# Four-layer gated cross-attention with expert feed-forwards: half-width value product and router bias on VectorE in layer 1, plain gathers with VectorE adds after layers 1 and 2, and three products of ones ahead of each head output of layer 1

## The reference

```python
x = x + tanh(g_xattn[l]) * xattn_l(layernorm(x), ctx_768)
x = x + tanh(g_ffn[l]) * ffn_l(layernorm(x))
```

## Time and profile before

| | us |
|---|---|
| median of 3 runs (lowest, highest) | 1220.69 (1220.15, 1220.71) |
| the profiled execution | 1213.56 |
| its span, first to last instruction | 1211.8 |
| TensorE busy (weight loads apart) | 1092.0 |
| VectorE, GpSimd, ScalarE busy | 876.1, 757.9, 577.1 |

### The profile page before, as it was taken

How to read it: one execution, slowest core, us unless ns; L and a number is a source line. 1 busy time by engine, 2 the same in 40 slices (tenths; PEclk the granted TensorE clock), 3 DMA queues, 4 the chain that set the end, 5 groups by cost and what they waited for, 6 DMA issues and landing times. The chain is left out here.

```text
span 1211.8 us, 23059 instructions
## 1 busy us (share of the span) xinstructions
PE 1092.0 (90%) x6989; PEld 772.5 (64%) x6990; DVE 876.1 (72%) x2216; ACT 577.1 (48%) x1248; POOL 757.9 (63%) x1010
## 2 busy tenths in 40 slices
PE   7999897889989999998899998999999999999553
PEld 5666563555556678956667766778976666666413
DVE  3899855888798668666678777666767777767496
ACT  2555432555455334444455544224435555554465
POOL 2455522764578864379998887853319988886213
PEclk7999996998898799999999999899999999999865
DMA  7996020000000015601111100023501111100002
GB/s 198 387 402 259 1 80 1 1 2 1 1 17 21 30 48 156 172 12 19 18 21 21 22 23 25 32 62 102 136 3 20 19 21 18 19 12 1 1 0 69
DMA packets 82304, 74.26 MB, mean 61 GB/s; under 512 B 9866, under 2 KB 69683, under 8 KB 82068
## 3 DMA queue, kind: packets, MB, share of 16 engines
q1 hardware_dynamic: 65300, 60.28, 15.6%
q0 software_dynamic: 16896, 12.64, 5.9%
HBM read 27.12 MB, written 45.78 MB: 60 GB/s over the span
## 5 line engine op out<-in xcount | busy, mean ns | idle before, releaser
L768 POOL TENSOR_TENSOR arena<-arena,zinv 128x1024 f32<-128x1024 f32 (+1 forms) x128 | 231.6, 1809 | 69.1 <-DVE zinv L1334 68.3
L1259 DVE TENSOR_REDUCE nmax<-S 128x16 f32<-128x1024 f32 (+1 forms) x128 | 138.9, 1085 | 94.5 <-PE S L1963 90.6
L1963 PEld LDWEIGHTS OX<-arena,pT 128*128 128x128 f32 x1280 | 151.6, 193 | 46.2 <-issue 45.6
L1963 PE MATMUL OX<-arena,pT 128*128 128x128 f32 x1280 | 166.3, 281 | 5.8 <-ACT pT L1043 5.8
L1963 PE MATMUL S<-arena,xT 128*128 128x512 f32 (+1 forms) x320 | 161.4, 603 | 1.1 <-ACT arena L1019 0.8
L1043 ACT ACTIVATE pT<-PT 128x512 f32<-128x512 f32 x224 | 124.5, 596 | 72.0 <-PE PT L2181 71.0
L2181 PE MATMUL PT<-ident,arena 128*128 128x128 f32 x896 | 130.1, 287 | 30.0 <-POOL arena L768 29.2
L2181 PEld LDWEIGHTS PT<-ident,arena 128*128 128x128 f32 x896 | 102.1, 145 | 67.6 <-POOL arena L768 54.4
L1319 DVE TENSOR_REDUCE zsum<-arena 128x16 f32<-128x1024 f32 (+1 forms) x128 | 137.8, 1076 | 0.0
L1310 DVE TENSOR_TENSOR arena<-S,nmax 128x1024 f32<-128x1024 f32 (+1 forms) x128 | 136.1, 1063 | 0.2 <-issue 0.2
L978 ACT ACTIVATE arena<-arena 128x1024 f32<-128x1024 f32 (+1 forms) x128 | 120.7, 943 | 7.1 <-DVE arena L1310 7.0
(11 more groups left out here) (357 smaller groups left out, 2326.7 us busy)
## 6 DMA issues: line engine op xcount, KB each, us to landing
x_sorted<-q_in SPq DMA_DIRECT2D x37, 387.0 KB, 5.3
y_sorted<-q_in SPq DMA_DIRECT2D x37, 384.0 KB, 5.3
arena<-x_sorted SPq DMA_DIRECT2D x62, 129.0 KB, 2.3
y_sorted<-arena SPq DMA_DIRECT2D x62, 128.0 KB, 2.1
x<-in_x SPq DMA_DIRECT2D x4, 512.0 KB, 8.2
out<-x SPq DMA_DIRECT2D x8, 256.0 KB, 2.3
x<-y_sorted,pos POOLq DMA_INDIRECT x96, 3.4
moe_flat<-in_L_gate_up_T SPq DMA_DIRECT2D x1, 1280.0 KB, 6.7
```

The source lines that it names most:

```text
L768: pool.tensor_tensor(pr, pr, z, ALU.mult).then_inc(s.probs_done, 1)
L1259: dve.tensor_reduce(nmax[:, p, 0:H], S[p][:, 0:W].rearrange("p (h k) -> p h k", h=H), AX.X, ALU.max, negate=True).then_inc(s.max_done, 1)
L1963: return pe.matmul(out, lhsT, rhs, start=start, stop=stop)
```

## The change

Layer 1's values are computed without the zero columns (128 columns instead of 2 x 128 per half); the zeros stand in a tile `v1` that GpSimd clears once, and two ScalarE instructions put the results in their places, each scaled by a column that is one on half of the partitions and zero on the other. The context is read from `ctxT` itself in layers 1 to 3, and GpSimd's copies to `ctx_b` stay in layer 0 alone. The router's bias product goes, and VectorE adds the bias for eight tiles at a time in a place ahead of the chain; the chain's first three instructions move one place on within their step. Ahead of the eight products of `heads1`, behind its first two waits, stand three products of ones into the same bank. The indirect DMAs become plain gathers into `y_rows` (four tiles deep, both issued two steps ahead), and VectorE adds the two rows of a tile to `x` three steps later, on both sides of its second norm.

```diff
-PICK_OPS, PICK0 = {1: 19, 2: 26}, {1: 20, 2: 96}
+PICK_OPS, PICK0 = {1: 20, 2: 26}, {1: 20, 2: 100}
...
+        wv1 = N[0:DC + 1, 0, :]
+        sides = sb("sides", [P, 2])
+        v1 = N[:, 8:13, :].rearrange("p h d -> p (h d)").rearrange("p (n x) -> p n x", n=2)
+        v1_filled = v1.rearrange("p n (a x) -> p n a x", a=2)[:, :, :, 0:4 * 32].rearrange("p n a (j q) -> p n a j q", j=4)
...
+        y_rows = moe2_flat[:, 3840:4864].rearrange("p (n k d) -> p n k d", n=4, k=2)
...
-            def add_first(l, n):
-                pool.indirect_dma_start(x[:, tile(l, n), :], None, y_sorted, bass.IndirectOffsetOnAxis(ap=pos[l][:, 0, n:n + 1], axis=0),
-                                        compute_op=ALU.add).then_inc(s.first_added[n % 4], 16)
-
-            def add_second(l, n):
-                pool.wait_ge(s.first_added[n % 4], 16 * (SPARSE // 4 * (l - 1) + n // 4 + 1))
...
+            def gather_first(l, n):
+                done(pool, s.sparse_added, SPARSE * (l - 1) + n - 4)
+                pool.indirect_dma_start(y_rows[:, n % 4, 0, :], None, y_sorted,
+                                        bass.IndirectOffsetOnAxis(ap=pos[l][:, 0, n:n + 1], axis=0)).then_inc(s.first_rows[n % 4], 16)
+
+            def gather_second(l, n):
+                pool.indirect_dma_start(y_rows[:, n % 4, 1, :], None, y_sorted,
+                                        bass.IndirectOffsetOnAxis(ap=pos[l][:, 1, n:n + 1], axis=0)).then_inc(s.second_rows[n % 4], 16)
...
-                    if r % 2 == 1 and is_batch(b):
+                    if a.l == 0 and r % 2 == 1 and is_batch(b):
...
-                            add_first(a.l - 1, t + 2)
+                            gather_first(a.l - 1, t + 2)
...
-                        if 0 <= t + 1 < SPARSE:
-                            add_second(a.l - 1, t + 1)
+                        if 0 <= t + 2 < SPARSE:
+                            gather_second(a.l - 1, t + 2)
...
             pool.wait_ge(s.out_done, TILES)
+            pool.memset(v1, 0.0).then_inc(s.v1_zeroed, 1)
...
-                            act.activation(V[:, ((r + 2) // 2) % 2, 0:2 * P], S[(r + 1) % 2][:, BANK:BANK + 2 * P], ACT.Copy).then_inc(s.v_evac, 2)
+                            if b == 0:
+                                act.wait_ge(s.sides_made, 4)
+                                act.wait_ge(s.v1_zeroed, 1)
+                            for e in range(2):
+                                act.activation(v1_filled[:, b % 2, :, :, 8 * e:8 * e + 8],
+                                               S[(r + 1) % 2][:, BANK:BANK + P].rearrange("p (a j e d) -> p e a j d", a=2, j=4, e=2)[:, e, :, :, :],
+                                               ACT.Identity, scale=sides[:, e:e + 1]).then_inc(s.v_evac, 1)
...
+            for e in range(2):
+                dve.memset(sides[0:64, e:e + 1], 1.0 - e).then_inc(s.sides_made, 1)
+                dve.memset(sides[64:P, e:e + 1], 1.0 * e).then_inc(s.sides_made, 1)
...
-                            dve.wait_ge(s.second_added[r], 16 * (SPARSE // 4 * (a.l - 2) + (t + 4 - RG) // 4 + 1))
+                            dve.wait_ge(s.sparse_added, SPARSE * (a.l - 2) + t + 4 - RG + 1)
...
+                    n = t - 1
+                    if a.l in (2, 3) and 0 <= n < SPARSE:
+                        xt, k = tokens(n + RG), SPARSE * (a.l - 2) + n + 1
+                        landed = 16 * (SPARSE // 4 * (a.l - 2) + n // 4 + 1)
+                        dve.wait_ge(s.first_rows[n % 4], landed)
+                        dve.tensor_tensor(xt, xt, y_rows[:, n % 4, 0, :], ALU.add).then_inc(s.half_added, 1)
                     if a.l:
                         second_norm()
+                    if a.l in (2, 3) and 0 <= n < SPARSE:
+                        dve.wait_ge(s.half_added, k)
+                        dve.wait_ge(s.second_rows[n % 4], landed)
+                        dve.tensor_tensor(xt, xt, y_rows[:, n % 4, 1, :], ALU.add).then_inc(s.sparse_added, 1)
...
+            def add_router_bias(L):
+                after()
+                mark(dve.tensor_tensor(L, L, router_b[:, :].unsqueeze(1).to_broadcast([P, RG, 8]), ALU.add))
...
                 if at == (0, 0):
                     dve.wait_ge(s.router_evac, RG * k + RG)
+                    add_router_bias(L)
+                elif at == (0, 1):
                     top_two(0, L)
...
                 L = lg[:, 24:32, :]
                 dve.wait_ge(s.router_evac, TILES)
                 dve.wait_ge(s.route_exp, 3)
+                add_router_bias(L)
                 for i in range(11):
...
-                        if a.l == 1:
-                            mm(OX[:, 3 * P:3 * P + 8], left, router_w[:, :], stop=False)
-                            ins = mm(OX[:, 3 * P:3 * P + 8], ones[0:1, :], router_b[0:1, :], start=False)
-                        else:
-                            ins = mm(OX[:, 3 * P:3 * P + 8], left, gwT[:, 1, :])
-                        ins.then_inc(s.router_done, 1)
+                        mm(OX[:, 3 * P:3 * P + 8], left, router_w[:, :] if a.l == 1 else gwT[:, 1, :]).then_inc(s.router_done, 1)
...
-                            ins = mm(S[(r + 1) % 2][64 * e:64 * e + 64, BANK:BANK + 2 * P], ctx_b[0:DC + 1, ((r + 2) // 2) % 2, :], v_blocks[:, e, :])
+                            ins = mm(S[(r + 1) % 2][64 * e:64 * e + 64, BANK:BANK + P], ctxT[0:DC + 1, b * KEYS:b * KEYS + KEYS], wv1)
...
                         done(pe, s.x_done, a.tile0 + t - 1)
+                        keep_busy(WARM_HEADS, GV)
                         for c in range(8):
                             if c % 4 == 0:
                                 done(pe, s.turned_evac, a.half0 + 2 * t + c // 4)
                             rows = slice(32 * (c % 4), 32 * (c % 4) + 32)
-                            ins = mm(GV[rows, 0:P], V[:, (r // 2) % 2, 32 * c:32 * c + 32], pT[:, r % 2, P * c:P * c + P],
+                            at = 32 * (c % 4) + 144 * (c // 4)
+                            ins = mm(GV[rows, 0:P], v1[:, (r // 2) % 2, at:at + 32], pT[:, r % 2, P * c:P * c + P],
...
+                                keys = ctx_b[0:DC + 1, par, :] if a.l == 0 else ctxT[0:DC + 1, batch_at(a.l, b) * KEYS:batch_at(a.l, b) * KEYS + KEYS]
+                                ins = mm(GV[64 * e:64 * e + 64, :].rearrange("p (c d) -> p c d", d=D), keys, rhs[:, e, :, :])
...
+WARM_HEADS = 3
...
-        "L1_v_blocks": np.zeros((DC + 1, 2, 8, 32), np.float32),
+        "L1_v_rows": np.concatenate([np.asarray(inputs["L1_xattn_wv"]), np.asarray(inputs["L1_xattn_bv"])[None, :]], axis=0),
```

More of the change, by code:

```diff
@@ L84 @@
 SCATTER_FROM = {1: 20, 2: 21}
-PICK_OPS, PICK0 = {1: 19, 2: 26}, {1: 20, 2: 96}
-LAST_PICK0 = {1: PICK0[1] + 3 * 19, 2: PICK0[2] + 3 * 26}
+PICK_OPS, PICK0 = {1: 20, 2: 26}, {1: 20, 2: 100}
+LAST_PICK0 = {1: PICK0[1] + 3 * 20, 2: PICK0[2] + 3 * 26}
 POS_OPS = 5
-PICKED = {1: 8, 2: 2}
-COUNTED = {1: 13, 2: 18}
-TAILED = {1: 19, 2: 26}
+PICKED = {1: 9, 2: 2}
+COUNTED = {1: 14, 2: 18}
+TAILED = {1: 20, 2: 26}
 RANK_PHASE = {1: 5, 2: 6}
@@ L166, in __init__ @@
         self.n_evac = sem("n_evac")
+        self.sides_made = sem("sides_made")
+        self.v1_zeroed = sem("v1_zeroed")
         self.attn_done = sem("attn_done")
@@ L234, in __init__ @@
         self.y_stored = [sem(f"y_stored{n}") for n in range(Y_RING)]
-        self.first_added = [sem(f"first_added{n}") for n in range(4)]
-        self.second_added = [sem(f"second_added{n}") for n in range(4)]
+        self.first_rows = [sem(f"first_rows{n}") for n in range(4)]
+        self.second_rows = [sem(f"second_rows{n}") for n in range(4)]
+        self.half_added = sem("half_added")
+        self.sparse_added = sem("sparse_added")
         self.rowsT_done = sem("rowsT_done")
@@ L708, in scatter @@
                                             token_rows[l][:, n, :], None).then_inc(sm, 16)
-            def add_first(l, n):
-                pool.indirect_dma_start(x[:, tile(l, n), :], None, y_sorted, bass.IndirectOffsetOnAxis(ap=pos[l][:, 0, n:n + 1], axis=0),
-                                        compute_op=ALU.add).then_inc(s.first_added[n % 4], 16)
-            def add_second(l, n):
-                pool.wait_ge(s.first_added[n % 4], 16 * (SPARSE // 4 * (l - 1) + n // 4 + 1))
-                done(pool, s.second_added[n % 4], 16 * (SPARSE // 4 * (l - 1) + n // 4) - 1)
-                pool.indirect_dma_start(x[:, tile(l, n), :], None, y_sorted, bass.IndirectOffsetOnAxis(ap=pos[l][:, 1, n:n + 1], axis=0),
-                                        compute_op=ALU.add).then_inc(s.second_added[n % 4], 16)
+            def gather_first(l, n):
[5 more added lines that the diff above has]
+                                        bass.IndirectOffsetOnAxis(ap=pos[l][:, 1, n:n + 1], axis=0)).then_inc(s.second_rows[n % 4], 16)
             def last_rows_stored(l):
@@ L1330, in step @@
                         routing(a.l, t, 3)
-                    if is_tile(n):
+                    if is_tile(t + 1):
```

(18 more changed lines are left out.)

12 lines of the change are left out of this document (5 added, 7 removed).

## The result

The changed kernel took 1203.92 us (median of four runs, 1201.04 to 1207.48) against 1220.42 before: a ratio of 0.9872, with a 95% interval of 0.9837 to 0.9908. The profiled execution took 1201.04 us, 12.5 less than the one of before (1213.56).

The account below looks back on a forecast made before the run. TensorE bound layer 2's settled steps, GpSimd its first tiles; in layer 1's attention no engine was full. -3.2 - 7.9 - 3.0 + 0.2 = -13.9 took 1213.56 to 1199.7, with 7.1 to the median 1206.8 us; range 1197 to 1221.

Parts of the forecast that it names:

- (g): Layers 2 and 3, GpSimd: plain gathers take 1.0 us instead of 1.641 and 1.584, -0.64 and -0.58 per step.
- (i): Layers 2 and 3, VectorE: two adds per tile, about 0.27 us each, fit in its slack; 0.
- R2: Rival, layers 2 and 3: a plain gather costs what the adding one does; 1216.3 us, chance 0.13.
- R4: Rival, layers 2 and 3: adds held 1.25 us by GpSimd's multiply, 0.7 per settled step; 1234.8 us, chance 0.08.
- (h): Layers 2 and 3, GpSimd: the copy of ctx_b goes, 0.238 us in every second step, -0.12 per step.
- (a): Layer 1, TensorE: three products of ones cost +0.74 us per even step at 2.4 GHz; odd steps counted 0.
- (c): Layer 1, TensorE: the router's bias product goes from the even path, -0.29 us.
- (e): Layer 1, ScalarE's value copy becomes two, 0, the next user a step away; memsets on GpSimd and VectorE 0 each.
- (b): Layer 1, TensorE: value products halved to 128 columns, -0.21 us in the even step, bounds 0 and 0.33.
- (d): Layer 1, clock: the light part shrinks by some 0.3 us, five of ten low-clock stretches go; -7.0 us.
- R1: Rival, layer 1: the clock does not recover, the light part keeps its idle time; 1213.8 us, chance 0.21.
- (f): VectorE: router bias as four instructions, only the last, at the start of layer 1's experts, counting; +0.2 us.

Follow-up runs that it names:

- the late adds: Changed kernel with both of VectorE's adds moved behind the reciprocal that starts GpSimd's multiply; median 1225.67 us, ratio 1.0034.
- the second profile: The changed kernel run once more, nothing altered, beside the others on one chip; median 1207.05 us, ratio 0.9882.

## Why the prediction was right, and where it was not

The time was right, by luck: two errors nearly cancel. Layers 2 and 3 were to give 10.9 us and gave 14.2 in the profiles; layer 1 was to give 3.2 and gave none. The profile itself was forecast at 1199.7 and took 1201.04; the 7.1 us carried from profile to median were not a property of the kernel, for the changed kernel's profile lies 2.9 below its median.

- **(g), (i), right.** Gathers of 1.0 us as forecast from the scatter's row; adds of 0.28, unheld, settled steps unchanged. R2 is out (0.99 to 1.04 us), and R4 is out for this kernel. Its mechanism, an add held by the multiply, is shown by the late adds; its price is not. R4 had one add held by 1.25 us in front of the reciprocal and 0.7 a step; the late adds stand behind the reciprocal, so that the x update and the next maximum wait, the hold is 1.67, and a step grows by 0.2 to 0.75.
- **(g) with (h), too small.** The nine steps gave 8.9 (7.9 forecast): TensorE, busy throughout, took 6.35, 6.85 and 6.46 us for the first three of these steps, and only then the alternation of 6.64 and 7.13 whose mean is the 6.89 of the sum. The rest of layer 2 gave 1.9 more that the sum didn't have: 1.1 in two steps that GpSimd's multiply held up in the kernel before (transposes at 699.05 and 706.63 us, waits of 0.25 and 0.68), and 0.7 in the last two steps, where the profile of before had 3.4 us at 1.2 GHz. Layer 3's rounding steps gave 4.6 and the step behind them took 1.15 back: 3.4 net, 3.0 forecast, as the sum had it: four steps and one behind them. (h) by itself gave 0.33, so naming it beside the gathers was more than it deserved.
- **(a) to (c), right in sign.** +0.11 a pair instead of +0.24: the ones cost 0.47, not 0.74, and the value and bias edits gave 0.36, not 0.50. The missed wait is in (e), which put ScalarE's two value copies at 0 because "the next user is a step away"; but the next scores wait for them, 0.33 us. The value products themselves are as much shorter as (b) said (0.65 to 0.44), yet without ones the scores come 2.58 us after the transposes; before, they came 2.53 after them (261.10 to 263.63):

```profile
263.63 1.13 PE L1963 MATMUL S<-arena,wd_all 64*128 64x512 f32 x4
```

So the wait eats all of (b), and the saving that is left is the bias product's. With the ones the wait is hidden, so they cost less than the 0.87 that they put the heads off by. The odd step's ones were free, as counted (5.20 before and after).

- **(d), the step that failed.** Five of ten falls were to go, -7.0. Against the same kernel with the gathers alone, the layer 1 edits moved the median by 1 us, inside the intervals, and the second profile had more time at the low level than before. The light part did shrink by some 0.3 (2.92 to 2.67), but not by the ones: without them it is 2.64, since the even step's ones lengthen it by what the odd step's take off (2.91 and 2.39 alone). Nor was it enough to keep half of the low time away: the two profiles have 23 and 44 us at 1.2 GHz, the one of before 35. R1's argument, that the products stand behind the light part, is what the runs bear out: without the ones the kernel is 13.5 us faster than with them, and with four products inside that part in their place 22.
- **(f) right:** 0.216 us for each of the four; only the last counts in the sum.

R1 was the rival with the right mechanism for layer 1; its 1213.8 was off by the larger gain of the gathers (3.3 us) and the smaller cost of (a) to (c) (2.0).

## What to carry to other kernels

Where a kernel's clock falls as it does here, filler work for it belongs into the idle time ahead of the fall: find the last idle stretch of the pipeline's period and put it just ahead of the wait that ends it, where it costs nothing; ahead of work on the path it is paid and may lengthen the very gap (2.91 us with ones in the even heads, 2.64 without). An accumulate in a gather DMA is paid in GpSimd's time, here 0.6 us each, so where GpSimd sets the step, plain gathers and an add on an engine with slack win, as long as a VectorE add with both inputs in SBUF stays clear of GpSimd's own instructions. A stage whose clock differs from execution to execution is judged by medians and by its full-clock step, not by one profile.

## What the runs showed of the hardware

- An indirect DMA that adds into SBUF holds GpSimd for 1.6 us per 128 rows, a plain one for 1.0; the same data otherwise.
- A VectorE add with both inputs in SBUF, started 0.08 us into a GpSimd multiply, took 1.956 us instead of 0.28, and the multiply kept its 1.89. The x update, which reads PSUM and SBUF, is not held beside the same multiply (0.29 us at 645.28 in the changed kernel).
- One kernel can lie at 0.94 or 0.89 of the clock through layer 1, 7.5 us apart, while its attention in layers 2 and 3 repeats to 0.02 us.
- Four 128x128 products of ones in an idle stretch of 0.87 us put off the transposes behind it by nothing (2.64 us behind the scores with and without them), and layer 1's PEclk was 0.99 instead of 0.94.
